# Second-sort keys computed in pieces inside the first eight walk steps, and biases ahead of the weight transposes, in a two-layer graph kernel

## The reference

```python
msg = h[edge_src] + relvectors[edge_rel]
red = jax.ops.segment_sum(msg, edge_dst, num_segments=h.shape[0])
x1  = layernorm(x + gru_cell(red, x, w_ih, w_hh, b_ih, b_hh))

deg   = segment_sum(ones, src)          # number of edges that leave each node
vals  = rsqrt(deg)[src] * rsqrt(deg)[dst]
h     = x1 @ W.T
out   = layernorm(x1 + segment_sum(vals[:, None] * h[dst], src))
```

## Time and profile before

| | value |
|---|---|
| median of three runs | 2138.76 us |
| profiled execution | 2137.24 us |
| its span | 2135.5 us |
| PE busy | 1912.2 us (90%) |
| DVE busy | 1709.5 us (80%) |
| ACT busy | 922.2 us (43%) |
| POOL busy | 1546.5 us (72%) |
| walk step 0 starts, walk step 8 starts | 45.17 us, 95.92 us |

### The profile page before, as it was taken

One profiled execution on the slowest core, in us unless ns is written; L12 is line 12 of the kernel. 1 busy time (PEld: TensorE's weight loads), 2 busy tenths in 40 slices (PEclk: granted clock), 3 DMA queues, 4 the chain that ended last, 5 costly groups with the idle time before them and its releaser, 6 DMA issues. The chain is left out here.

```text
span 2135.5 us, 41955 instructions
## 1 busy us (share of the span) xinstructions
PE 1912.2 (90%) x9416; PEld 1470.3 (69%) x9416; DVE 1709.5 (80%) x3028; ACT 922.2 (43%) x3074; POOL 1546.5 (72%) x1633
## 2 busy tenths in 40 slices
PE   4799989789999989999997999998989999877997
PEld 3567767467777766777775788776767776656886
DVE  6499989999999968888876899788767787544676
ACT  3100000146666635444343998477725786000123
POOL 7767777777777776777766777777777777777771
PEclk8999999899999999999999999999999999999999
DMA  6355555444444455566664333333333333333334
GB/s 170 110 159 169 170 170 169 135 129 140 145 144 144 143 157 173 183 196 190 185 183 130 100 107 106 101 106 107 107 105 106 107 106 106 107 106 105 107 106 139
DMA packets 125298, 289.62 MB, mean 136 GB/s; under 512 B 30214, under 2 KB 60374, under 8 KB 124908
## 3 DMA queue, kind: packets, MB, share of 16 engines
q0 software_dynamic: 77504, 211.67, 34.6%
q10 hardware_dynamic: 37120, 64.87, 8.8%
q1 hardware_dynamic: 10444, 10.38, 1.6%
HBM read 254.81 MB, written 38.40 MB: 137 GB/s over the span
## 5 line engine op out<-in xcount | busy, mean ns | idle before, releaser
L1816 PE MATMUL ps<-rows,onehot 128*128 x5632 | 1336.2, 391 | 117.3 <-SPq L475 47.5
L1816 PEld LDWEIGHTS ps<-rows,onehot 128*128 128x128 f32 x5632 | 1062.2, 192 | 326.0 <-issue 156.9
L617 POOL DMA_INDIRECT rows<-in_x_dram,tidx x815 | 782.7, 960 | 278.0 <-issue 236.1
L638 POOL DMA_INDIRECT rows<-gdram,tidx x784 | 742.8, 947 | 258.9 <-issue 241.2
L952 DVE TENSOR_TENSOR sums<-sums,ps 128x256 f32 x390 | 162.7, 417 | 240.6 <-PE ps L1816 220.8
L911 DVE SCALAR_TENSOR_TENSOR onehot<-tkey,node_p,ps 128x512 f32<-128x512 f32 x400 | 295.6, 739 | 14.6 <-issue 10.6
L969 DVE TENSOR_TENSOR sums<-ps,sums 128x800 f16<-128x800 f32 (+1 forms) x156 | 215.4, 1413 | 1.2 <-issue 1.2
L859 DVE SCALAR_TENSOR_TENSOR onehot<-tkey,node_p,ps 128x1024 f32<-128x1024 f32 x152 | 193.1, 1270 | 2.5 <-DVE steps_i L839 1.0
L1570 ACT ACTIVATE wT<-wT,a 128x208 f16<-128x208 f16 x312 | 116.1, 454 | 122.2 <-DVE wT L853 122.2
L1515 ACT COPY sums<-ps 128x256 f32<-128x256 f32 x49 | 18.2, 372 | 342.3 <-PE ps L1872 342.3
L1531 ACT ACTIVATE sums<-sums 128x50 f32<-128x50 f32 x416 | 95.0, 230 | 106.2 <-DVE sums L1033 106.2
(11 more groups left out here) (312 smaller groups left out, 2036.2 us busy)
## 6 DMA issues: line engine op xcount, KB each, us to landing
xpd<-sums ACTq DMA_DIRECT2D x48, 384.0 KB, 3.3
sums<-xpd ACTq DMA_DIRECT2D x48, 384.0 KB, 3.6
rows<-in_x_dram,tidx POOLq DMA_INDIRECT x815, 2.8
rows<-gdram,tidx POOLq DMA_INDIRECT x784, 2.7
xt<-in_x_dram ACTq DMA_DIRECT2D x80, 128.0 KB, 2.4
gdram<-in_x_dram ACTq DMA_DIRECT2D x5, 1250.0 KB
gdram<-sums ACTq DMA_DIRECT2D x48, 128.0 KB
out_dram<-sums SPq DMA_DIRECT2D x5, 896.0 KB
```

What stands on the lines that cost most here:

```text
L617: pool.indirect_dma_start(rows[0:z, slot * RS:slot * RS + D], None, x[:, :], bass.IndirectOffsetOnAxis(ap=tidx[0:z, column:column + 1], ax ...
L638: pool.indirect_dma_start(rows[:, slot * D:slot * D + D], None, gdram[:, :], bass.IndirectOffsetOnAxis(ap=tidx[:, column:column + 1], axis ...
L1816: prod = M.matmul(ps[:, h, 0:width], onehot[:, u % U, k, :], rows[:, bass.ds(at + k * stride, width)], start=(k == 0), stop=(k == q - 1))
```

## The change

The ten expressions of `prepare_second` become five pieces, run by the walk of the first eight steps at steps 2, 3, 5, 6 and 7, each ahead of that step's `hots` and `evict`. `tiles_needed` moves to step 2. Two waits are added inside them: at step 3 for the bias matmuls (since `a32` is overwritten), at step 5 for the first twelve transposes (since `lo1` lies over the first weights). After step 7 VectorE waits for the last transpose in place of running the block.

On TensorE the bias matmuls move from behind step 7 to behind step 0, and each batch of four transposes moves one step later (steps 1 to 7). On ScalarE the bias copies come ahead of the weight copies. The number of instructions stays the same on every engine.

```diff
-            def prepare_second():
-
-                step(V.tensor_copy(lo1, tidx[:, 0:C]))
-                step(V.scalar_tensor_tensor(mask, tkey[:, :], float(PAD_KEY), m16[:, :], ALU.is_lt, ALU.subtract))
-                step(V.tensor_tensor(scan, tkey[:, :], mask, ALU.mult))
-                step(V.scalar_tensor_tensor(lo1, lo1, -float(PAD_KEY), mask, ALU.add, ALU.mult))
-                step(V.tensor_scalar(lo1, lo1, float(PAD_KEY), None, ALU.add))
-                floor_of(hi1, lo1, P)
-                step(V.scalar_tensor_tensor(lo1, hi1, -float(P), lo1, ALU.mult, ALU.add))
-                floor_of(a32[:, :], scan, 8)
-                step(V.scalar_tensor_tensor(pos, a32[:, :], -8.0, scan, ALU.mult, ALU.add))
-                step(V.scalar_tensor_tensor(b32[:, :], pos, float(P), lo1, ALU.mult, ALU.add))
+            def prepare_second(j):
+
+                if j == 2:
+                    tiles_needed()
+                    step(V.scalar_tensor_tensor(mask, tkey[:, :], float(PAD_KEY), m16[:, :], ALU.is_lt, ALU.subtract))
+                    step(V.tensor_tensor(scan, tkey[:, :], mask, ALU.mult))
+                if j == 3:
+                    dve.wait_ge(s_bias_mm, 3)
+                    floor_of(a32[:, :], scan, 8)
+                    step(V.scalar_tensor_tensor(pos, a32[:, :], -8.0, scan, ALU.mult, ALU.add))
+                if j == 5:
+                    dve.wait_ge(s_wtr, 2 * G3 // P)
+                    step(V.tensor_copy(lo1, tidx[:, 0:C]))
+                    step(V.scalar_tensor_tensor(lo1, lo1, -float(PAD_KEY), mask, ALU.add, ALU.mult))
+                    step(V.tensor_scalar(lo1, lo1, float(PAD_KEY), None, ALU.add))
+                if j == 6:
+                    floor_of(hi1, lo1, P)
+                    step(V.scalar_tensor_tensor(lo1, hi1, -float(P), lo1, ALU.mult, ALU.add))
+                if j == 7:
+                    step(V.scalar_tensor_tensor(b32[:, :], pos, float(P), lo1, ALU.mult, ALU.add))
...
-            walk(0, FIRST)
+            walk(0, FIRST, prepare_second)
 
             dve.wait_ge(s_edges, 144)
             dve.wait_ge(s_bias, 3)
-            tiles_needed()
-            prepare_second()
+            dve.wait_ge(s_wtr, BLOCKS_EACH * (FIRST - 1))
...
             def beside_first(j):
 
-                if j < FIRST - 1:
-                    turn_weights(j * BLOCKS_EACH, (j + 1) * BLOCKS_EACH)
+                if j == 0:
+                    biases()
                 else:
-                    biases()
+                    turn_weights((j - 1) * BLOCKS_EACH, j * BLOCKS_EACH)
+                if j == FIRST - 1:
+                    pe.wait_ge(s_wcp, len(blocks) + len(TURN))
+                    clear(4, SUB // 2 * B)
+                    clear(5, SUB // 2 * B)
```

More of the change, by code:

```diff
@@ L1493, in _ @@
                     A.copy(dest[:, a:z], ps[:, bank + c, 0:z - a]).then_inc(s_keys, 1)
+            for m, (bank, first, size) in enumerate(((4, 0, 2 * D), (5, 2 * D, D), (7, 3 * D, D))):
+                act.wait_ge(s_bias_mm, m + 1)
+                A.activation(bias[:, first:first + size], ps[:, bank, 0:size], ACT.Identity,
+                             scale=0.5 if m == 2 else 1.0).then_inc(s_bias, 1)
             at = 0
@@ L1499, in _ @@
                 at += 1
[L1500 to L1503, removed]
             def load_x(t, k, rws):
@@ L1747, in turn_weights @@
             def turn_weights(first, last):
-                pe.wait_ge(s_w, 96)
+                pe.wait_ge(s_bias, 3)
                 for at in range(first, last):
@@ L1754, in biases @@
             def biases():
-                pe.wait_ge(s_wcp, len(blocks) + len(TURN))
+                pe.wait_ge(s_w, 96)
                 one = ones[0:1, :]
@@ L1761, in biases @@
                 M.matmul(ps[:, 7, 0:D], one, brow[1][:, 2 * D:G3], start=True, stop=True).then_inc(s_bias_mm, 1)
-                pe.wait_ge(s_bias, 3)
-                clear(4, SUB // 2 * B)
-                clear(5, SUB // 2 * B)
             def beside_first(j):
-                if j < FIRST - 1:
-                    turn_weights(j * BLOCKS_EACH, (j + 1) * BLOCKS_EACH)
-                else:
-                    biases()
+                if j == 0:
+                    biases()
+                else:
+                    turn_weights((j - 1) * BLOCKS_EACH, j * BLOCKS_EACH)
[3 more added lines that the diff above has]
+                    clear(5, SUB // 2 * B)
             def count(ready, done):
```

## The result

| kernel | median (runs) | before on the same chip | ratio, 95% interval |
|---|---|---|---|
| changed | 2134.13 us (14) | 2138.30 us (14) | 0.998 [0.9973, 0.9987] |
| changed, measured again beside the last experiment | 2131.75 us (8) | 2137.98 us (12) | 0.9974 [0.9963, 0.9984] |

By the ratios the change makes the kernel 4.2 us faster in the first measurement (2.8 to 5.8) and 5.6 in the second (3.4 to 7.9; its two medians differ by 6.2). The forecast was 6.0. The runs of the changed kernel lie 5.0 and 6.0 us apart in the two measurements. One execution of each measurement is profiled: "the first" took 2135.41 us (span 2133.7), "the second" 2128.97 us (span 2127.2). Read together they show what the change gives in every execution and what only one of them has.

The account below looks back on a forecast made before the run. The walk and nearly as slow gathers were taken to bound the kernel together, TensorE waiting for the block of keys; -5.6 (gathers) - 0.4 (lead) = -6.0 us from the 2138.76 median gave 2132.8 us, range 2129.3 to 2137.5.

Parts of the forecast that it names:

- The block leaves the path: Behind step 7: VectorE's first counting one-hots come at 92 to 93 us, and TensorE's 7.37 us wait is gone.
- Rival C: First steps run at the lower clock, 21 us over seven steps, making the kernel slower, 2150.6 us; chance 0.07.
- Steps 1 to 7 are 1.9 us later: TensorE's order: bias matmuls (2.84 us) ahead of step 1 delay steps up to 7 by 1.9 us, returned behind step 7.
- The walk gains 9.5 us at step 9: Step 9 starts at 105.0 us in place of 114.49; with the slow 5.22 us start the gain is 7.3.
- The gathers cap it: After GpSimd's 5.89 us wait vanishes, gathers gain 5.58 us and no more for 300 us, limiting the walk.
- Rival A: The walk's whole gain of 9.5 us arrives at the end, 2129.3 us; chance 0.06.
- The size of the cap, 5.58: GpSimd's gather behind the vanished ring wait is issued at 113.58 us in place of 119.16, 5.58 us earlier.
- The lead left at step 48, 0.4: At step 48 the walk adds 0.4 us from its 4.41 us lead over the gathers; estimates 0.2 to 1.1.
- The sum: Gathers' 5.6 us plus 0.4 us of lead by step 48 move everything behind: -6.0 us, median 2132.8 us.
- the forecast proper: The whole kernel's median falls at 2131 to 2133.5 us, around 2132.8; chance 0.60.
- Rival B: Less arrives, 2133.5 to 2138 us: short instructions slow GpSimd more, or a wait at step 48 costs 2.95 us of clock; chance 0.27.
- The stretched gathers: VectorE's one-input instructions slow GpSimd's gathers, 1.84 us over five; kept the same under gathers between 63 and 85 us.

Follow-up runs that it names:

- the two edits: Changed kernel with TensorE's and ScalarE's old order, `a32`, `pos`, `b32` behind step 7, and the five `gdram` copies 48 steps later: 2129.96 us, ratio 0.9965 to the kernel before.

## Why the prediction was right, point by point

**The block leaves the path.** Right: first counting one-hots at 93.60 and 93.07 (said: 92 to 93), no 7.37 us wait, no stage at the lower level between 60 and 92 us. Rival C did not occur.

**Steps 1 to 7 are 1.9 us later.** The totals, 2.2 in the first execution and 1.7 in the second, are near it by luck. Step 0 started 0.56 and 0.38 us later and ran 0.53 and 0.18 longer, before changed code; the change itself adds 1.1 to 1.2. The term had set the bias matmuls (2.84) against the transposes (0.96) and left out that TensorE idled 0.74 us between the transposes and step 1, which it does not behind the bias matmuls. The pieces on VectorE cost nothing, as said: TensorE's idle before steps 2 to 7 is 0.71 to 0.81 us (0.71 to 0.87 before). Step 8 came at 95.54 and 94.97, said 95.6 to 96.2.

**The walk gains 9.5 us at step 9.** Measured 9.07 and 11.49. The distance from the counting to step 9 is 105.42 - 102.34 = 3.08, as taken from later steps. The spread is step 8 itself, 6.97 us in one execution and 5.12 in the other.

**The gathers cap it.** Right, and the point on which all hung. The walk's 9 to 11.5 us were 4.8 and 6.1 at step 48. Rival A (9.5 us arrive) fell with both executions, and with the kernels whose walk gained 12.6 to 18.7 us and whose time did not follow. That the second execution's 2128.97 us is near A's number is luck: 2.2 of its 8.3 us came behind step 48. The rows that show it without a theory are the two with the delay on GpSimd.

**The size of the cap, 5.58.** The step "the wait vanishes and the gathers gain 119.16 - 113.58" was mis-sized in the first execution: 4.71. GpSimd's restart at the ring's first wait came at 52.85 in place of 51.77, since step 0 started later and took 6.28 us in place of 5.75. Against that stand 0.41 us less of stretched gathers; the last 0.2 is spread thinly over the 48 gathers in between. Until step 48 the gathers lost another half a microsecond. In the second execution, with the restart at 52.32, it is 5.34. The forecast took the restart of the one profiled execution of before as given; over the profiles here it lies between 50.78 and 53.01.

**The lead left at step 48, 0.4.** Too low, and the wrong place in the changed kernel. What the walk had over the gathers' gain was 0.67 us in the first and 0.82 in the second execution, but step 48 did not wait in either; the walk was held at step 39 and at step 47. Step 39 started 7.6 us behind the last issue of its group and step 47 8.8 (351.38 less 342.61), each with a copy to `gdram` issued beside them (290.19 and 342.81), so the sum was near with the holding step wrong. Where the copies are gone, step 48 is the one that waits, and with the two edits it gave 1.16. The shortest distance from the last issue to the product was 3.25 us, not 4.2. The bound from the median landing, 1.1, was the better one.

**The sum.** The two terms together were forecast as 6.0 and measured as 4.84 and 6.13 at step 48. The prediction said that whatever is gained by step 48 moves everything behind it; that step was too simple. From step 48 to the last wait near 1350 us the first execution lost 2.2 us and the second gained 2.2. A part is the clock behind waits (above), the rest was not traced to a cause. So a median is explained to no better than 2 us, and that the medians of the second measurement differ by 6.2, close to 6.0, says less than the rows up to step 48. The median of the first measurement, 2134.13, lies outside the 2131 to 2133.5 of the forecast proper, in the stretch given to rival B.

**Rival B.** Half of it occurred. The first execution is in its range. The clock was lost at a wait for gathers, at step 39 (6.52 us), but there it was lost before as well (6.88), and newly at step 30, where both executions waited over 3 us and took 5.62. At step 48, where it was priced, no product ran slowly in the two executions; it did in the changed kernel with late copies (6.61). How often that happens in the runs that were not profiled is open.

**The stretched gathers.** The step "the block's instructions with one input slow GpSimd" failed in its attribution, though its size, 1.84 us kept, was near: 1.43 over four gathers of the first execution (60.38, 67.06, 77.52 and 87.97). Two of these (67.06 and 77.52), one that was not stretched, and what VectorE did beside them:

```profile
65.81 0.95 POOL L617 DMA_INDIRECT rows<-in_x_dram,tidx  x1 [0.31 <-issue]
67.06 1.39 POOL L617 DMA_INDIRECT rows<-in_x_dram,tidx  x1 [0.30 <-issue]
...
77.52 1.37 POOL L617 DMA_INDIRECT rows<-in_x_dram,tidx  x1 [0.30 <-issue]
```

```profile
65.34 0.59 DVE L684 TENSOR_SCALAR a<-a 128x832 f32<-128x832 f32 x1
65.97 0.59 DVE L685 TENSOR_SCALAR a<-a 128x832 f32<-128x832 f32 x1
66.60 1.03 DVE L717 SCALAR_TENSOR_TENSOR sums<-a,sums 128x832 f32<-128x832 f32 x1
...
77.47 0.59 DVE L722 TENSOR_SCALAR sums<-sums 128x832 f32<-128x832 f32 x1
```

What counts is what runs at the moment the gather starts. At 67.06 the instruction with two inputs of 66.60 has 0.57 us to go, and the gather takes 0.44 more than its 0.95. At 77.52 one with one input has 0.54 to go: 0.42 more. At 65.81 only 0.12 are left, and nothing is added. In all twelve profiles 93 gathers from 50 us on start within an instruction of 832 columns. 46 are stretched, each by what was left of the instruction less 0.12 to 0.13 us; 34 found 0.15 us or less left and lost at most 0.03; 13 started within 0.04 us of the instruction's start and lost nothing. So a gather that comes second waits for the rest of VectorE's instruction, with one input or two. The reverse does not hold: the instructions of 65.97 and 66.60 start 0.16 and 0.79 us into the gather of 65.81 and take their usual 0.59 and 1.03 us. The most that any of these instructions lost with a gather ahead of it is 0.23 us (the cast at 75.57 of the first execution, 0.81 us). The rule of the Trainium skill (SBUF — State Buffer, "Who interferes with whom") is that whoever issues first has the shared ports for its whole instruction, and that an instruction with two inputs in SBUF contends with a GpSimd instruction that reads SBUF. The trace agrees where VectorE comes first, and not where the gather does. The forecast took the small mean (0.37 us) as speaking against a full block. It was one, met part-way: with 1.25 us between gathers and 0.59 or 1.03 us per instruction, most gathers meet only a part of one.

## What to carry to other kernels

When a wait is removed from one of two engines that feed each other through a ring, the gain up to the tightest place behind it is the other engine's own wait (less what that engine starts late) plus the lead at that place, not what the first engine gained. Further on, waits and clocks added or took up to 2.2 us here. Both are rows of the trace: the other engine's wait for a free place near the removed one, and the smallest distance from an issue to its use behind it. Delaying the suspected engine by less than its wait, in both kernels, and reading the rows at both places, is the sharpest test here. And where runs differ by as much as the change is worth, profile the changed kernel twice before explaining a difference late in the trace.

## What the runs showed of the hardware that was not expected

- With a large copy beside them the small gathers landed late. Step 39 of the changed kernel started 7.6 us after the last issue of its group (301.24 less 293.65) with the copy of 290.19 beside it; in the kernel with the two edits, whose copies come 48 steps later, 3.33 us were enough (296.33 less 293.00, no wait). Not every wait was the copy's: step 30 of the changed kernel waited 3.44 us with the copies in place and 4.21 without. The median landing of these gathers is 2.8 us.
- Work just ahead of a wait did not raise the clock for the product behind it: with 1.31 us of transposes issued at 39.86 and a wait of 4.25 us, step 0 took 6.16 us, where a step at the upper level takes 3.93.
- The same wait can leave either level behind it. In the kernel with the two edits, three products that had waited 1.57 to 2.06 us for landings took 3.93 us, and one behind 2.52 us in the changed kernel with late copies as well; in the kernel before with late copies one that had waited 1.97 us took 5.62.
